# Four graph layers on one core: nodes without incoming edges placed first, rows scattered by place

## What is computed

```
x = layernorm(x + gin(x))      # (x + sum of sources) @ W1, relu, @ W2
x = layernorm(x + sage(x))     # mean of sources @ W_l + x @ W_r, batch norm, relu, + x
x = layernorm(x + gat(x))      # two attention convolutions (4 heads of 256), then a product
x = layernorm(x + gcn(x))      # degree-scaled sums, product, batch norm, gelu, + x
```

## Time and profile before

| | |
|---|---|
| median of 3 runs | 3914.8 us (3913.59 to 3915.11) |
| the profiled execution's own time | 3912.85 us |
| its span, first to last instruction | 3911.1 us |
| PE busy | 3419.3 us, 87% of the span |
| DVE busy | 2155.2 us, 55% |
| ACT busy | 1463.1 us, 37% |
| POOL busy | 1452.1 us, 37% |
| bytes moved by DMA | 821.41 MB, mean 210 GB/s |

### The profile page before, as it was taken

The page is one execution under the profiler, slowest core; times in us unless marked ns, Lnnn a source line. Parts: engine busy times, 40 slices in busy tenths (PEclk is TensorE's granted clock), DMA queues, the critical chain, the costliest instruction groups (busy, mean ns, idle before and its releaser), DMA issues. The chain is left out here.

```text
span 3911.1 us, 55988 instructions
## 1 busy us (share of the span) xinstructions
PE 3419.3 (87%) x19416; PEld 2074.1 (53%) x19416; DVE 2155.2 (55%) x3972; ACT 1463.1 (37%) x2580; POOL 1452.1 (37%) x1231
## 2 busy tenths in 40 slices
PE   4669998989969999886999999998859999859964
PEld 3234443545637666664666666666635555315543
DVE  7257775845554444276543443413758888406667
ACT  1323332533324444353332332322534444233357
POOL 2345553225422222253333323212536666343312
PEclk7789999989979999997999999999979999979976
DMA  2667774656659999597978878944957777375558
GB/s 82 201 184 198 196 201 146 201 172 228 227 195 259 279 274 281 180 280 213 256 192 204 204 194 198 200 119 146 280 209 259 262 261 262 123 231 186 174 167 275
DMA packets 624227, 821.41 MB, mean 210 GB/s; under 512 B 378374, under 2 KB 378374, under 8 KB 622032
## 3 DMA queue, kind: packets, MB, share of 16 engines
q1 hardware_dynamic: 556880, 598.37, 50.3%
q0 software_dynamic: 67200, 221.25, 20.1%
HBM read 470.83 MB, written 263.59 MB: 188 GB/s over the span
## 5 line engine op out<-in xcount | busy, mean ns | idle before, releaser
L326 PE MATMUL bank<-w_lo,t_r_hi 128*128 128x344 f16 (+1 forms) x2560 | 838.8, 328 | 0.0
L327 PE MATMUL bank<-w_hi,t_r_hi 128*128 128x344 f16 (+1 forms) x2560 | 838.6, 328 | 0.0
L325 PE MATMUL bank<-w_hi,w_lo 128*128 128x344 f16 (+1 forms) x2240 | 716.7, 320 | 49.8 <-DMA w_lo<-g_row_lo 31.3
L2415 DVE SCALAR_TENSOR_TENSOR t_z<-w_lo,t_z 128x256 f32<-128x256 f32 x320 | 243.5, 819 | 396.4 <-DMA w_lo<-h 393.4
L326 PE MATMUL bank<-w_lo,w_hi 128*128 128x344 f16 (+1 forms) x1280 | 419.6, 328 | 0.0
L327 PE MATMUL bank<-w_hi 128*128 128x344 f16 (+1 forms) x1280 | 419.4, 328 | 0.0
L2389 POOL TENSOR_TENSOR t_row_lo<-t_r,t_row_hi 128x1024 f16<-128x1024 f32 x80 | 174.9, 2187 | 509.8 <-ACT t_row_hi L2436 509.8
L327 PEld LDWEIGHTS bank<-w_hi,t_r_hi 128*128 128x128 f16 x2560 | 250.9, 98 | 168.8 <-issue 0.8
L326 PEld LDWEIGHTS bank<-w_lo,t_r_hi 128*128 128x128 f16 x2560 | 250.9, 98 | 162.5 <-issue 0.6
L325 PE MATMUL bank<-w_hi 128*128 128x344 f16 x960 | 298.3, 311 | 21.8 <-DMA w_hi<-t_row_lo 19.2
L325 PEld LDWEIGHTS bank<-w_hi,w_lo 128*128 128x128 f16 x2240 | 219.3, 98 | 181.7 <-issue 50.8
(11 more groups left out here) (345 smaller groups left out, 6732.2 us busy)
## 6 DMA issues: line engine op xcount, KB each, us to landing
w_lo<-h SPq DMA_DIRECT2D x160, 512.0 KB, 5.7
h<-b_wide SPq DMA_DIRECT2D x80, 516.0 KB, 9.6
h<-w_hi SPq DMA_DIRECT2D x80, 516.0 KB, 2.9
sum_gat<-a_out SPq DMA_DIRECT2D x80, 514.0 KB
l_x<-x SPq DMA_DIRECT2D x40, 1024.0 KB, 9.1
sum<-e_out SPq DMA_DIRECT2D x120, 256.0 KB
g_x<-in_x SPq DMA_DIRECT2D x20, 1024.0 KB, 5.6
x<-g_y SPq DMA_DIRECT2D x20, 1024.0 KB, 5.1
```

What stands on the lines that cost most here:

```text
L325: pe.matmul(out, s_lo, m_hi, start=(k == 0), stop=False)
L326: pe.matmul(out, s_hi, m_lo, start=False, stop=False)
L327: mm = pe.matmul(out, s_hi, m_hi, start=False, stop=last)
L2415: ins = v.scalar_tensor_tensor(out=z[u][:, s, cols], in0=hrow[:, s, cols], scalar=z[u][:, s, HC + h:HC + h + 1], in1=z[u][:, s, cols], op0 ...
```

## The change

Nodes get places: those without incoming edges come first, in their order, then the others in theirs. Setup computes each node's place (`places_of_nodes`). The first layer still works in node order, and scatters its finished rows to their places in `x1` (`to_places`), four indirect DMAs by POOL instead of one store by SP. All later stages work in the order of places, and the output stage scatters its rows back to node order. Tables by node and by place are written to DRAM and looked up by indirect DMA: in `gin_stage` the sources' places (`look_up`, 40 in all), in `edge_product_stage` 80 scatters of the 12-byte rows of `by_place` (two after each gather), in `sage_stage` 40 look-ups ahead of the first gather of sums, in the place of the 40 that stood there. Since the first `d.early` = 8 groups of places then hold no node with an edge, `sage_stage` makes no gathers, transposes or additions of sums for them. Apart from that, `score_rows` uses the transposing form of the product with the identity.

```
+        self.early = max(nodes - edges, 0) // (2 * GROUP) * 2
...
+    def places_of_nodes(dve):
...
+        n = st.mark(v.tensor_tensor(off_place[:], node_f[:], ranks[:, 0:K], ALU.subtract))
...
+        n = st.mark(v.tensor_tensor(kn.place_i[:], off_place[:], place_up[:], ALU.subtract))
...
+        pe.wait_ge(alone_steps.sig.sem, alone_steps.sig.at(3))
+        pe.wait_ge(table_ready.sem, table_ready.at(B))
+        pe.matmul(alone_total_ps, alone[:], kn.ones[:], start=True, stop=True).then_inc(products.sem, 1)
         pe.wait_ge(ties_ready.sem, ties_ready.at(B))
...
@@ edge_product_stage, gpsimd
+        def store_by_place(k):
+            pool.indirect_dma_start(dram["by_place"], bass.IndirectOffsetOnAxis(ap=kn.place_at_i[:, k:k + 1], axis=0),
+                                    kn.by_place[:, k, :], None, bounds_check=d.padded - 1, oob_is_err=False)\
+                .then_inc(table_out.sem, 16)
...
+            for k in range(t * per, min((t + 1) * per, d.blocks)):
+                store_by_place(k)
+        pool.wait_ge(table_out.sem, table_out.at(16 * d.blocks))
@@ edge_attention_stage, score_rows
-                mm = pe.matmul(row_ps[u][:, h, :], spread[u][:, h, :], kn.ident[:], start=True, stop=True)
+                mm = pe.transpose(row_ps[u][:, h, :], spread[u][:, h, :], kn.ident[:])
...
+def to_places(kn, pool, rows, g, s, landed):
+
+    pool.indirect_dma_start(kn.dram["x1"], bass.IndirectOffsetOnAxis(ap=kn.place_i[:, g * S + s:g * S + s + 1], axis=0),
+                            rows, None, bounds_check=kn.d.padded - 1, oob_is_err=False).then_inc(landed.sem, 16)
+
+
+def look_up(kn, pool, out, at, t, landed):
+    pool.indirect_dma_start(out[:, t, :], None, kn.dram["by_node"],
+                            bass.IndirectOffsetOnAxis(ap=at[:, t:t + 1], axis=0),
+                            bounds_check=kn.d.padded - 1, oob_is_err=False).then_inc(landed.sem, 16)
...
@@ gin_stage
-            if g:
-                store(g - 1)
...
-            pool.wait_ge(stored[u].sem, stored[u].at(i * 16))
+            pool.wait_ge(placed[u].sem, placed[u].at(i * 16 * S))
...
+        def store(g):
+            i, u = divmod(g, 2)
+            pool.wait_ge(rows_out[u].sem, rows_out[u].at(i * S + S))
+            for s in range(S):
+                to_places(kn, pool, y[u][:, s, :], g, s, placed[u])
...
+            store(g)
+            for t in range(g * per, min((g + 1) * per, d.tiles)):
+                look_up(kn, pool, kn.src_by, kn.src_at_i, t, found)
+        pool.wait_ge(found.sem, found.at(16 * d.tiles))
+        nc.gpsimd.tensor_copy(kn.src_i[:], kn.src_by[:, :, 1]).then_inc(sources.sem, 1)
+        pool.wait_ge(sources.sem, sources.at(1))
+        for u in range(2):
+            pool.wait_ge(placed[u].sem, placed[u].at(16 * S * H))
@@ sage_stage, gpsimd
+        for t in range(T):
+            look_up(kn, pool, dst_by, kn.dst_at_i, t, found)
+        for g in range(E, G):
             load_sums(g)
@@ sage_stage, vector
-                dve.wait_ge(a_turned.sem, a_turned.at(g * 4 + m + 1))
                 dve.wait_ge(biased.sem, biased.at(g * 4 + m + 1))
-                v.tensor_tensor(h[u][:, m, :], ta[m % 2][:], h[u][:, m, :], ALU.add).then_inc(h_done.sem, 1)
-                dve.wait_ge(h_done.sem, h_done.at(g * 4 + m + 1))
+                if g >= E:
+                    dve.wait_ge(a_turned.sem, a_turned.at((g - E) * 4 + m + 1))
+                    v.tensor_tensor(h[u][:, m, :], ta[m % 2][:], h[u][:, m, :], ALU.add).then_inc(h_done.sem, 1)
+                    dve.wait_ge(h_done.sem, h_done.at((g - E) * 4 + m + 1))
@@ sage_stage, tensor
-                turn_sums(g, m)
+                if g >= E:
+                    turn_sums(g, m)
@@ output_stage
-            sp.wait_ge(rows_out.sem, rows_out.at(g * S + S))
-            sp.dma_start(node_rows(dram["out"], *divmod(g, 2)), x[g])\
-                .then_inc((first_stored if g < B else stored).sem, 16)
...
+        def store(g):
+            pool.wait_ge(rows_out.sem, rows_out.at(g * S + S))
+            for s in range(S):
+                pool.indirect_dma_start(dram["out"],
+                                        bass.IndirectOffsetOnAxis(ap=kn.node_i[:, g * S + s:g * S + s + 1], axis=0),
+                                        x[g][:, s, :], None, bounds_check=d.padded - 1, oob_is_err=False)\
+                    .then_inc((first_stored if g < B else stored).sem, 16)
...
+            if g:
+                store(g - 1)
+        store(G - 1)
+        pool.wait_ge(first_stored.sem, first_stored.at(16 * S * B))
+        pool.wait_ge(stored.sem, stored.at(16 * S * (G - B)))
```

More of the change, by code:

```diff
@@ L62, in __init__ @@
         self.slots = self.none + 1
+        self.early = max(nodes - edges, 0) // (2 * GROUP) * 2
         self.last_real = nodes - (self.groups - 1) * GROUP
-        assert self.sent >= nodes and 0 < self.last_real <= GROUP
+        assert self.sent >= nodes and self.early >= 2 and 0 < self.last_real <= GROUP
         assert self.blocks <= P and self.tiles <= P
@@ L363, in __init__ @@
         self.degrees = take("target_degrees", 2)
+        self.places = take("places_known", 2)
 def setup_stage(kn, mem, tables):
@@ L456, in setup_stage @@
     vec_done = take("vec_done", 2)
-    consts = Steps(take("const_steps", 13))
+    consts = Steps(take("const_steps", 14))
     split = Steps(take("split_steps", 4))
@@ L461, in setup_stage @@
     ties_ready = take("ties_ready", B)
-    products = take("setup_products", 7)
-    COUNTED, ROWS_SUMMED, BASED, TIED, SORTED_DONE, ENDS_DONE, RIM_COUNTED = range(1, 8)
+    products = take("setup_products", 9)
+    COUNTED, ROWS_SUMMED, BASED, ALONE_SUMMED, TIED, RANKED, SORTED_DONE, ENDS_DONE, RIM_COUNTED = range(1, 10)
     blocks_counted = take("blocks_counted", B)
@@ L466, in setup_stage @@
     row_ready = take("row_ready", 1)
-    turned = take("turned", Q)
+    turned = take("turned0", Q)
     turned_ready = take("turned_ready", Q)
@@ L545, in scalar @@
             act.copy(high_turned[0:K, c * 4 * P:(c + 1) * 4 * P], wide_ps[c % 2][0:K, :]).then_inc(turned_ready.sem, 1)
+        act.wait_ge(products.sem, products.at(ALONE_SUMMED))
+        act.copy(alone_total[0:K, :], alone_total_ps).then_inc(ranked.sem, 1)
+        act.wait_ge(products.sem, products.at(RANKED))
+        act.copy(ranks[:], ranks_ps).then_inc(ranked.sem, 1)
     def vector(dve):
@@ L812, in tensor @@
         ins.then_inc(products.sem, 1)
+        pe.wait_ge(ranked.sem, ranked.at(1))
+        pe.matmul(ranks_ps[:, 0:K], above, alone[:], start=True, stop=False)
+        pe.matmul(ranks_ps[:, 0:K], alone_total[0:K, :], above[0:K, 0:K], start=False, stop=True)
+        pe.matmul(ranks_ps[:, K:K + 1], alone_total[0:K, :], kn.ones[0:K, 0:1], start=True, stop=True)\
+            .then_inc(products.sem, 1)
         pe.wait_ge(table_ready.sem, table_ready.at(B))
@@ L1668, in gin_stage @@
     x_in = pair("x_in", 16 * H)
-    sum_in = pair("sum_in", 16 * S * H, software=True)
+    sum_in = [take(f"sum_in{u}_0", 16 * S * H, software=True) for u in range(2)]
     z_ready = pair("z_ready", H * S)
@@ L1681, in gin_stage @@
     rows_out = pair("rows_out", S * H)
-    stored = pair("stored", 16 * H)
+    placed = pair("placed_out", 16 * S * H, software=True)
+    found = take("dinv_in", 16 * d.tiles, software=True)
+    sources = take("sources_ready", 1)
     def sync(sp):
@@ L1710, in sync @@
                 load_x(g + 2)
-            if g:
-                store(g - 1)
             if g + 1 < G:
                 turn(g + 1)
-        store(G - 1)
-        for u in range(2):
-            sp.wait_ge(stored[u].sem, stored[u].at(16 * H))
     def gpsimd(pool):
@@ L1864, in sage_stage @@
     x_in = pair("x_in", 16 * H)
-    sum_in = pair("sum_in", 16 * S * H, software=True)
-    dinv_in = take("dinv_in", 16 * T, software=True)
+    sum_in = [take(f"sum_in{u}_0", 16 * S * (H - d.early // 2), software=True) for u in range(2)]
+    table_in = take("dinv_out", 16)
+    found = take("dinv_in", 16 * T, software=True)
+    tables = take("slot_steps", 3)
     negated = take("negated", 4)
+    dst_by = kn.buffer(mem, "l_dst_by", [P, T, 2], F32)
+    E = d.early
     bias_ready = take("bias_parts", 1)
     turned = take("turned0", 4 * G)
-    a_turned = take("turned1", 4 * G)
+    a_turned = take("turned1", 4 * (G - d.early))
     hi_done = take("hi_done", 4 * G)
```

184 lines of the change are left out of this document (123 added, 61 removed).

## The result

The changed kernel takes 4041.65 us (4036.74 to 4052.78, 4 runs), the kernel before 3914.95; the ratio is 1.0326 (1.0311 to 1.0341). It is slower by some 127 us; I had forecast 34.5 us, with a range that ended at 3994. The sign is right, the size is not, and the result lies outside the range. The profiled execution has a span of 4041.3 us where it was 3911.1.

The account below looks back on a forecast made before the run. PE was taken to bound gin_stage and sage_stage, with nearly all added work on POOL. Terms 0.5 + 0 + 18 + 9 + 7 - 14 + 0 + 14 = +34.5 gave 3949 us; range 3922 to 3994, likeliest case 3929 to 3968.

Parts of the forecast that it names:

- Setup, +0.5: Setup: counting nodes without edges puts one small f32 product on PE ahead of a DVE step; +0.5 us, 0 to 1.
- gin_stage, POOL +0, DMA +18: gin_stage groups: POOL's six more issues just fit, +0; the later 1 MB store delays the transposes, +18 us, 0 to 28.
- The step on the collision: gin_stage: the store, moved among the transposes, delays the second transposition, so PE waits 0.93 us more per group.
- gin_stage, end, +9: End of gin_stage: four scatters and two look-ups delay the next stage by 9 us, or 15 if a queue drain follows their landing.
- edge_product_stage, +7: Edge products: three POOL issues take 4.1 us against a tile's 3.83, so the last gather lands late; +7 us, 0 to 16.
- sage_stage, -14: sage_stage: 16 transposes of sums fewer in each of 8 groups save PE 14 us, or 8 if x is late.
- output_stage, +14: output_stage: four scatters exceed POOL's idle time by 0.42 us per group, +8, plus a later end; +14 us, 10 to 40.
- Attention, 0: Attention: the transposing form shortens score_rows, but PE's wait for DVE's a_lhs lengthens by the saved time; 0.
- Rival A: Scatters and look-ups cost POOL 1.38 us and more each, in gin_stage, edge products and output; +83, 3998 us; chance 0.17.
- B: Rival: PE's clock falls in attention without the identity product's longer form; +30, 3979 us; chance 0.11.
- C: Rival: all added work is hidden but the ends, and only the output's queue is late; +8, 3923 us; chance 0.15.
- D: Rival: PE, not DVE, sets attention's pace, so each of 80 tiles gains 0.54 us; total -8.5, 3906 us; chance 0.07.

Follow-up runs that it names:

- e_weights_after: Changed kernel, with DVE's preparation of later weights and SP's loads for it behind the 40 tiles of edge_product_stage, not one piece per tile; 4152.45 us, one run.
- s_long_ops: Changed kernel, but in sage_stage POOL computes for some 2.2 us after every eighth look-up, waiting for nothing; 4005.86 us.
- s_paced: Changed kernel, but in sage_stage POOL issues two of the 40 look-ups per group, paced by PE, not all ahead of the sums' gathers; 4003.89 us.
- g_lookups_last: Changed kernel, with all 40 look-ups of gin_stage behind its last group and score_rows back in the product form of before; 4096.88 us.
- no_row_scatters: Changed kernel, one by_place scatter per edge tile, the rest and sage_stage's look-ups spread over its groups, SP's contiguous stores in gin_stage and output_stage; 3913.8 us.

## Why the prediction was wrong

*Setup, +0.5.* Setup and first sums together grew by 3.7 us (202.9 against 199.1; 200.5 to 203.2 in the experiments' profiles). It is small, and no run takes it apart.

*gin_stage, POOL +0, DMA +18.* 21.4 us came (25.1 less 3.7), so the sum was right within 4 us. The step on the collision is borne out: the second transposition landed later, and PE's wait for it went from nothing to 1.42 us in the group shown and to 1.09 in the mean of 17, where I had worked out 0.93. What I had not seen is that the bias waits for the scatters' landing; it shows up at the same size, and no run here separates the two. So the size is borne out, and that the transposition alone makes it is not.

*gin_stage, end, +9.* 14.3: the variant that I had named for +15, the queue's drain behind the landing, is what happened. POOL was idle for 9.08 us behind its drain.

*edge_product_stage, +7.* This step failed. That POOL's queue would set the pace was right, but I priced three issues at 4.1 us a tile and they took 4.64: 1.20 us an issue in the mean instead of about 1.07, because of DVE's preparation of weights, of which the sum says nothing. Without that work three issues are 3.97 us, which by itself would be +5.5. But e_weights_after shows that this was not to be had either: with issues of that length the others stalled, and the tiles took 196.2 us. What came is +36.1. With one scatter per tile the term is +3.0.

*sage_stage, -14.* Right for the groups (12.1 us) and for the stage without the stall (-13.2 in s_long_ops). Wrong for the change as made: "The 40 look-ups take POOL 52 us; the first sums are wanted in group 8" asks only who waits for the look-ups. Nobody does. The row itself costs 44 us (320.9 against 276.6 in s_paced). This is the larger failed step: the sum put the effect of POOL's long row on PE, DVE and ACT at nothing, without a reason.

*output_stage, +14.* The mechanism was right, the size was off: 0.76 us per group instead of 0.42, since I had left out the pause of 0.50 us ahead of the first scatter (14.4 us over 19 groups, where I had 8), and 11.2 at the end, where I had 6: the execution ended 9.9 us after the last scatter's issue began (4031.37), not 4.9. +25.6.

*Attention, 0.* -0.6 for all between `sage_stage` and the output. In part that is luck: the two attention stages took 186.6 and 188.5 us where it was 185.7 twice, and the stage between them 4.6 less; no run says why. PE was busy for 18 to 20 us less in each of the two, and they were not shorter for it, which is what the step had said.

The range of the likeliest case, 3929 to 3968, is narrower than its bounds allow: all the lower bounds together give about 3920. It changes nothing here, since even A's 3998 was too low.

Rival A (dear issues, 3998) named the right places, and in the edge products its longer issues are in the trace; but e_weights_after shows the loss without them, and in `sage_stage`, where the issues took 1.00 us, it has no part. The Trainium skill (GPSIMD Engine Reference, Specifications) says that POOL shares its SBUF interfaces with VectorE, in contention where DVE has two SBUF inputs or a two-port mode. By that rule the trace agrees in part: in the changed kernel's edge products the 10 issues beside DVE's `w_lo<-f_stage,w_hi` (two SBUF inputs) took 2.1 us in the mean, the 28 beside `e_z_lo<-bank,e_z_hi` (one input from PSUM) 1.01. But the 8 beside `f_prod<-f_stage,f_rows`, with two SBUF inputs as well, took 1.01 too. B fell: the granted clock in the two attention stages is 0.92 and 0.90, before 0.92 in both, and with the product form of before (g_lookups_last) their times are the same. C's 3923 needed what no_row_scatters leaves out, and D fell with the attention stages' times. None of the rivals was the one that decided.

## What to carry to other kernels

A queue with room does not take a long row of indirect DMAs for nothing: count how many are issued without a break, and pace them by the engine that computes, or put some two microseconds of other work behind every eighth. Ask of each moved transfer what it collides with and who waits for its landing; in `gin_stage` the order of scatters and gathers on one queue was worth 80 us. And read a stage group by group: the forecast gain of 14 us was there, under a stall of 44.

## What the hardware showed that I had not expected

- A long row of POOL's indirect DMAs, one each 1.3 us, stalls PE, DVE and ACT: matmuls 2.8 us apart, waits of up to 27 us for work long done, next to no transfer under way. The first late product came 11 us, nine issues, into the row (twice); rows of 16 stalled, rows of eight with a break hardly. It came with rows of 4 and 8 bytes, and in the edge products beside 12-byte scatters, in the kernel before as in the changed one, and lasts about as long as the row.
- What is held up is open. The trace's records of semaphore updates are incomplete in the edge products of the changed kernel (34 updates for 40 tiles' products; 40 in the kernel before), so the path of the records may be part of it. Every run here was recorded, so none shows whether the stall is there without the recording.
- The Trainium skill (NOTIFIC — the notification-queue block, Overflow: three behaviours, one of which stalls the engine) says that the block that writes such records holds its producers back rather than lose one inside. No run here shows whether that is what happened.
- An indirect scatter costs POOL the same as a gather where DVE doesn't stretch it: the medians are 1.02 us for rows of 12 bytes, 1.01 and 0.97 for rows of 2 KB (`x1` and `out`), and 1.00 for the gathers of `sage_stage`.
